# Two modulation loads ahead of the key strips, combined modulations inside the first slot, and the second MLP's rounding and weight split moved

## What is computed

```
x = L0(x, cond): h = LN(x)*(1+scale)+shift; GQA with rope, sparse mask, 16 heads; x + y @ Wo.T
x = L1(x, cond): x + attn(ada_rms(x)) @ Wo.T, 8 query heads, one key head;
                 x + (silu(h @ Wg.T) * (h @ Wu.T)) @ Wd.T,  h = ada_rms(x)
x = L2(x, cond): x + attn(LN(x)*(scale1+1)+shift1) * gamma1, 16 heads, cosine scores;
                 h = gelu((LN(x)*(scale2+1)+shift2) @ Wfc1.T + bfc1)
                 x + (h @ Wfc2.T + bfc2) * gamma2
x = L3(x, cond): x + silu(LN(experts(x))*(1+scale)+shift) @ out_W + out_b
```

## Time and profile before

| | us |
|---|---|
| median of 3 runs | 2375.68 |
| their range | 2372.73 to 2376.46 |
| the profiled execution | 2368.46 |
| its span | 2366.7 |

### The profile page before, as it was taken

One profiled execution on the slowest core, in us unless ns is written; L12 is line 12 of the kernel. 1 busy time (PEld: TensorE's weight loads), 2 busy tenths in 40 slices (PEclk: granted clock), 3 DMA queues, 4 the chain that ended last, 5 costly groups with the idle time before them and its releaser, 6 DMA issues.

```text
span 2366.7 us, 33414 instructions
## 1 busy us (share of the span) xinstructions
PE 2231.2 (94%) x13442; PEld 1492.4 (63%) x13442; DVE 1169.9 (49%) x2498; ACT 1039.6 (44%) x2433; POOL 286.2 (12%) x239
## 2 busy tenths in 40 slices
PE   7789999999999999999999889999999899999998
PEld 2355556545555688888887656565655578888633
DVE  2355455445456434434333467566577454444322
ACT  3365556444345211111113376666676552222473
POOL 2332122112111100010000000001010110000021
PEclk8799999999999999999999999999999999999999
DMA  7411010000000103120002211111110100100001
GB/s 235 158 41 40 24 54 15 28 23 17 25 32 27 58 1 107 45 67 19 27 6 98 81 54 54 37 55 46 45 37 19 54 5 31 36 1 1 1 19 53
DMA packets 60715, 104.93 MB, mean 44 GB/s; under 512 B 10624, under 2 KB 25488, under 8 KB 60560
## 3 DMA queue, kind: packets, MB, share of 16 engines
q1 hardware_dynamic: 60208, 102.37, 13.0%
q0 software_dynamic: 352, 0.42, 0.1%
HBM read 77.07 MB, written 10.49 MB: 37 GB/s over the span
## 4 chain that ended last, share of the span: by engine, by line
PE 84%; ACT 7%; DVE 6%; SPq 1%; DMA 1%; issue 1%; POOL 1%; DVEq 0%; ACTq 0%; POOLq 0%
PE banks L1300 36%; PE banks L408 22%; PE banks L749 6%; PE banks L741 5%; PE banks L765 4%; ACT sb_Pr L888 2%; PE banks L269 1%; PE banks L976 1%; DVE sb_hN L368 1%; ACT sb_PT L893 1%; PE banks L634 1%; PE banks L642 1%; DVE sb_Pr L836 1%; PE banks L960 1%; PE banks L789 1%
## 5 line engine op out<-in xcount | busy, mean ns | idle before, releaser
L1300 PE MATMUL banks<-sb_HH,sb_Ws 128*128 128x512 f32 x1536 | 489.5, 392 | 7.6 <-DVE sb_HL L1188 7.6
L1300 PEld LDWEIGHTS banks<-sb_HH,sb_Ws 128*128 128x128 f32 x1536 | 289.6, 189 | 71.1 <-issue 8.1
L1300 PE MATMUL banks<-sb_hidH,sb_Ws 128*128 128x512 f32 x1024 | 330.3, 392 | 0.4 <-DVE sb_x L1371 0.4
L888 ACT ACTIVATE sb_Pr<-sb_Pr,sb_nmax 128x512 f32<-128x512 f32 (+4 forms) x512 | 291.6, 576 | 20.9 <-DVE sb_nmax L836 20.8
L1300 PE MATMUL banks<-sb_HL,sb_Ws 128*128 128x512 f32 x768 | 299.8, 390 | 0.0
L893 ACT ACTIVATE sb_PT<-banks 128x512 f32<-128x512 f32 (+2 forms) x320 | 144.1, 497 | 291.5 <-PE banks L749 232.5
L843 DVE COPY sb_PT<-banks 128x512 f32<-128x512 f32 (+2 forms) x320 | 168.0, 564 | 169.5 <-PE banks L749 112.0
L749 PEld LDWEIGHTS banks<-sb_ident,sb_Pr 128*128 128x128 f32 x1536 | 168.4, 142 | 125.9 <-issue 35.8
L749 PE MATMUL banks<-sb_ident,sb_Pr 128*128 128x128 f32 x1536 | 213.5, 281 | 18.4 <-DVE sb_A L876 5.0
L1300 PEld LDWEIGHTS banks<-sb_hidH,sb_Ws 128*128 128x128 f32 x1024 | 192.2, 188 | 43.6 <-issue 2.3
L1300 PE MATMUL banks<-sb_hidL,sb_Ws 128*128 128x512 f32 x512 | 199.3, 389 | 0.0
(11 more groups left out here) (164 smaller groups left out, 3178.3 us busy)
## 6 DMA issues: line engine op xcount, KB each, us to landing
sb_ring<-split_units SPq DMA_DIRECT2D x48, 512.0 KB, 3.2
sb_ropet<-sb_R SPq DMA_DIRECT2D x70, 128.0 KB, 2.1
sb_staged<-in_L_cond_Wfc SPq DMA_DIRECT2D x16, 512.0 KB, 4.4
sb_wada<-in_L_cond_Wada SPq DMA_DIRECT2D x6, 1024.0 KB, 5.4
split_units<-sb_unitpair SPq DMA_DIRECT2D x12, 512.0 KB, 2.9
sb_x<-in_x SPq DMA_DIRECT2D x4, 1024.0 KB, 9.1
sb_staged<-in_L_cond_Wg SPq DMA_DIRECT2D x8, 512.0 KB, 3.6
sb_staged<-in_L_cond_Wu SPq DMA_DIRECT2D x8, 512.0 KB, 4.6
```

What stands on the lines that cost most here:

```text
L888: ins = e.activation(prob, prob if s.biased else k.bank(n % 4)[:, 0:s.width(u)], ACT.Exp, bias=s.stat(k, k.nmax, b, u), scale=-1.0 if s.bi ...
L1300: mm = e.matmul(bank, lhsT, rhs, start=i == 0, stop=i == len(mats) - 1)
```

## The change

1. SP loads blocks 8 and 9 ahead of the key strips.
2. The seven `comb` operations and the rounding of `headsel` leave the end of `lead` and are spread over slot 0 as a fourth stream of side work (`sums`). Slot 0 has eight beats more.
3. Batch 1's rounding for the second MLP (`beats((pair2, 1))`) moves from the MLP's first parts to the `closing` of the last attention slot, two beats at each of two points.
4. The second MLP's weight chunk is split in two pieces of 1024 columns, staged in four buffers that are loaded and freed singly. Chunk 1's two pieces stand in two parts, `(2, 4)`. The last slot has one beat more.

```diff
-                ins = e.tensor_copy(high, s.staged[index % 2][:, 0:w])
+                ins = e.tensor_copy(high, s.staged[index % len(s.staged)][:, 0:w])
...
-        staged2 = [place("staged20", 25600, [P, 2048]), place("staged21", 4096, [P, 2048])]
+        staged2 = [place(f"staged2{i}", o, [P, 1024]) for i, o in enumerate((25600, 26624, 4096, 5120))]
...
-            [(ada, 0, "act", "scales", 0)] + [(ada, 0, "dve", "comb", i) for i in range(len(combs))] +             [(headmatrix, 0, "dve", "round", 0)]
+            [(ada, 0, "act", "scales", 0)]
+        sums = [[(ada, 0, "dve", "comb", i)] for i in range(len(combs))] + [[(headmatrix, 0, "dve", "round", 0)]]
...
-            sides01.append(([] if m else pre(1, 0)) + first + among(late, rest, pre(m + 2, 0)) + [[]])
+            sides01.append(([] if m else pre(1, 0)) + first +
+                           among(late, rest, pre(m + 2, 0), *([] if m else [sums])) + [[]])
...
-        mlp2 = mlp(2, False, split2, staged2, [(0, 2 * C * HC)], norm2b, pair2, [("proj2", B - 1, "mm", 11)],
+        mlp2 = mlp(2, False, split2, staged2, [(0, C * HC), (C * HC, 2 * D)], norm2b, pair2, [("proj2", B - 1, "mm", 11)],
...
+        second = beats((pair2, 1))
...
-                           closing=[[], first[0], [], first[1]])
-        hidden2 = fold(parts, (0, 1, extras(0) + extras(1)), (0, 2, beats((pair2, 1))), (0, 4, beats((post2, 3))),
-                       (2, 3, mlp2.split(1)), (1, start[2] + 1, beats((norm2b, 2))),
+                           closing=[[], first[0] + sum(second[:2], []), sum(second[2:], []), first[1]])
+        hidden2 = fold(parts, (0, 1, extras(0) + extras(1)),  (0, 4, beats((post2, 3))),
+                       (2, 4, mlp2.split(1)), (1, start[2] + 1, beats((norm2b, 2))),
...
-            for n in (6, 7):
+            for n in range(6, 10):
                 load_block(n)
...
-                    for n in range(8, len(blocks)):
+                    for n in range(10, len(blocks)):
                         load_block(n)
...
                 if j >= 2:
-                    done("mlp2", 0, "low", j - 2)
+                    done("mlp2", 0, "low", 2 * j - 4)
...
+                if j >= 2:
+                    done("mlp2", 0, "low", 2 * j - 3)
```

More of the change, by code:

```diff
@@ L1507, in conditioned_stack @@
         l_ring = [sem(f"l_ring{i}") for i in range(4)]
-        l_m = [sem(f"l_m{i}") for i in range(2)]
+        l_m = [sem(f"l_m{i}") for i in range(4)]
         s_zero = sem("s_zero")
@@ L1834, in conditioned_stack @@
                           lambda b: [("out3", b - 3, "mm", C - 1)] if b >= 3 else
-                          mlp_down("mlp2", LAST - 3) + [("mlp2", 0, "low", NCH - 1)])
+                          mlp_down("mlp2", LAST - 3) + [("mlp2", 0, "low", 2 * NCH - 1)])
         norm3 = SideNorm("norm3", y3, y3, combc(3), combc(4), eps5[:, 0:1],
@@ L1852, in among3 @@
             return sum(among(*parts), [])
-        l_m_at, seen = {1: [], 2: []}, [0, 0]
-        for layer, loads in ((1, [2, 1] * NCH), (2, [2] * NCH)):
+        l_m_at, seen = {1: [], 2: []}, [0] * 4
+        for layer, count, loads in ((1, 2, [2, 1] * NCH), (2, 4, [1, 1] * NCH)):
             for n, m in enumerate(loads):
-                seen[n % 2] += 16 * m
-                l_m_at[layer].append(seen[n % 2])
+                seen[n % count] += 16 * m
+                l_m_at[layer].append(seen[n % count])
         def up(W, layer_ups):
@@ L1869, in mlp @@
             heads = f"heads{n}"
-            return Mlp(f"mlp{n}", gated, W, pieces, staged, lambda i: (l_m[i % 2], l_m_at[n][i]),
+            return Mlp(f"mlp{n}", gated, W, pieces, staged, lambda i: (l_m[i % len(staged)], l_m_at[n][i]),
                        up(W, 2 if gated else 1), down(W, (2 if gated else 1) * C * HC), norm, pair,
@@ L2094, in _ @@
                     done(*values_end("heads2", 2)[0])
[L2095 to L2098 removed]
+                e.dma_start(staged2[2 * (j % 2)][:].rearrange("p (c m) -> p c m", c=C),
+                            rows("L2_cond_Wfc1")[:, :, j * HC:(j + 1) * HC]).then_inc(l_m[2 * (j % 2)], 16)
+                if j >= 2:
+                    done("mlp2", 0, "low", 2 * j - 3)
+                e.dma_start(staged2[2 * (j % 2) + 1][:].rearrange("p (t m) -> p t m", t=2),
+                            rows("L2_cond_Wfc2")[:, 2 * j:2 * j + 2, :]).then_inc(l_m[2 * (j % 2) + 1], 16)
                 if j == 3:
```

6 lines of the change are left out of this document (1 added, 5 removed).

## The result

The changed kernel took 2358.58 us (median of 6 runs, 2346.25 to 2362.16) against 2373.69 us of the kernel before on the same chip (6 runs). The ratio is 0.9933, with a 95% interval from 0.9918 to 0.9948: 15.9 us less. A second set of six runs on another chip gave 0.9946 (0.9934 to 0.9958), 12.8 us less. The forecast was 2355.8 us, 19.9 us less, a ratio of 0.9916. Both times lie inside the range of 2348 to 2366, and both gains fall short of the forecast, by 4.0 and 7.1 us; the second, 12.8, lies outside the 15 to 25 that the forecast had for itself, and nearer to the 12 of rival (a). Two executions of the experiments are far off the others, 4410 us for p3_round and 2866 us for p1_e_empty_beats, and are in none of the ratios.

The account below looks back on a forecast made before the run. TensorE, busy 94%, was taken as the bound, so only its waits and low-clock stretches count. Gains 14.0 + 0.25 - 0.5 + 5.1 + 1.0 = 19.9 us, from 2375.68 to 2355.8 us; range 2348 to 2366, the forecast's own 2351 to 2361.

Parts of the forecast that it names:

- rival (a): Start gives back more: slow strips, late block 11, or slot 0 bound by GpSimd and dearer sums; gain about 12, 14%.
- Part 1: At the start, TensorE's 10.79 us wait for block 8 goes, block 10 waits 1.3 us; gain 14.0, bounds 11 to 15.3.
- Part 2: First maximum's 3.35 us wait moves to batch 1's mean, gain 0.25; slot 0 loses 0.5, between gain 2 and loss 3.
- signs of being wrong: Strips issued beyond 66 us, low clock after 90, larger wait ending slot 3, or 100 us gain shrunk at 180.
- Part 3: At the attention's end, HL1 wait and clock give 6.8 us, less 1.7 at batch 2's variance; net 5.1, between 3 and 6.8.
- The later wait: In the second MLP, batch 3's wait hangs on batch 2's chain and moves with it; no size of its own given.
- Part 4: In the attention, smaller split pieces shorten the 2.43 us stall; gain 1.0, between gain 2.4 and loss 1; MLP costs nothing.
- the lower bound: In the attention, batch 0's roundings shifted by one beat can make maxima wait for ScalarE; within the loss of 1 us.
- the price of cutting an operation in two: On VectorE, two split pieces cost 0.6 us more than one whole by the rows, 0.3 by the skill's fixed cost.
- The clock rival (d): TensorE's clock stays at 1.2 GHz through slot 0 because of many short waits; +40 us, time 2396, 4%.

Follow-up runs that it names:

- p3_round: Kernel before with only batch 1's rounding moved to the attention's end, chunk 1 still split as one piece: 0.9969 of before, -7.4 us.
- p1_e_empty_beats: Kernel before with blocks 8 and 9 loaded ahead of the strips and eight empty beats in slot 0, sums left ahead of the first maximum: 0.9965, -8.3 us.
- p12: Kernel before with the early loads of blocks 8 and 9 and the sums spread over slot 0, nothing else: 0.9961 of before, -9.3 us.
- after_again: The whole changed kernel run once more, on another chip beside the kernel before: 0.9946 of before.
- p13: Kernel before with the early loads of blocks 8 and 9 and batch 1's rounding moved, without the spread sums and split pieces: 0.9907, -22.1 us.
- p2_sums: Kernel before with only the seven sums and the rounding spread over slot 0, with its added beats: 1.0032 of before, +7.6 us.
- p1_loads: Kernel before with only the loads of blocks 8 and 9 put ahead of the key strips: 0.9941 of before, -14.0 us.

## Why the prediction was right, and where not

**Part 1, right in each step.** Blocks 8 and 9 were issued from 47.47 us on by a queue with nothing else to do, the strips started at 52.15, no later than before, and took 10.93 us. Block 10 was issued behind them at 63.13 and ran at 68.63 after a DMA wait of 1.46 us; the forecast was 1.3 us and 70.0, which is the same once the 1.4 us are taken off by which this execution was ahead at 50 us. Block 11 did not wait. Forecast 14.0, measured 13.9 in the ledger; the 14.0 of the medians has 5 us either way and could not tell 14 from 10. What the forecast did not have is the lower clock behind block 10, which takes 1.5 of the 13.9 us in some executions, the changed kernel's profile among them. (The prediction's 64.51 + 5.4 is 69.91, where it has 69.97; nothing hangs on it.)

**Part 2, the step that failed.** The forecast had a gain of 0.25 at the first maximum and a loss of 0.5 in slot 0, "between a gain of 2 and a loss of 3". The first half is shown: the wait went over to the mean, at 85.84 where 86 was written. The second half was mis-sized. Over the 704 matmuls of slot 0 the changed kernel loses 1.6 us against part 1 alone, p12 3.5 and after_again 6.4, and part 2 alone loses 6.9 against the kernel before; in the times part 2 alone costs 7.6 us (5.0 to 10.2). The prediction did name the mechanism, "TensorE reaches the variance before GpSimd has it", and then let "projection work done earlier" pay for it. It doesn't pay. With empty beats TensorE idles 16.44 us in slot 0 against 14.38 with part 1 alone, 2.06 us more, and the new wait at the variance is 2.01 us: in sum, the work that is pulled forward shortens no other wait. And the clock, which costs little where TensorE waits anyway, is paid in full here.

Two of the signs of being wrong that the prediction lists came: the gain had shrunk between 100 and 180 us, and the clock was low after 90 us (0.50 from 90 to 97 us). The second tells nothing, since p13 without part 2 has the same 0.50 there and loses nothing by it. Rival (a), "the start gives back more", had four clauses. The chain of slot 0 bound by GpSimd is the true one. Sums of over 1 us on VectorE came in part, 0.75 to 1.22 us each where 0.37 was taken from a row of six, but TensorE does not wait for them. Strips issued slowly and block 11 late did not come.

**Part 3, right, and somewhat better.** HL1's last low part was done at 1835.64 in the changed kernel, ten microseconds before TensorE came to it, on VectorE:

```profile
1834.36 1.28 DVE L1188 TENSOR_TENSOR sb_HL<-sb_hN,sb_HH 128x512 fp32r<-128x512 f32 x2
```

The forecast was 6.8 us before the variance wait and 5.1 after it. Alone, with the variance wait unchanged, part 3 gave 7.4 (4.3 to 10.4), and the ledger of p3_round steps by 7.1 between 1850 and 1890. The split's piece ahead of the centring, on VectorE in the changed kernel, against the earlier trace rows:

```profile
1859.14 0.69 DVE L1340 CAST sb_Ws<-sb_staged 128x1024 fp32r<-128x1024 f32 x1
1859.86 1.23 DVE L1344 TENSOR_TENSOR sb_Ws<-sb_staged,sb_Ws 128x1024 fp32r<-128x1024 f32 x1
1861.00 2.47 DVE L348 TENSOR_TENSOR sb_hN<-sb_x,banks 128x512 f32<-128x512 f32 x4
```

cost 1.65 us at the variance (2.60 against 0.95) where 1.7 was written. The forecast booked it under part 3; it is part 4's. The later wait, for batch 3's HL3, did move with the chain and kept its size: 2.24 us, 2.23 before.

**Part 4, mis-sized.** Forecast a gain of 1.0; the attention's side of it gave 0.2 us in the ledger, and with the variance wait part 4 is a loss of about 1.4 by the profiles. The times show no difference (0.9991 to 1.0014, from 2 us gained to 3 us lost). The stall of 2.43 us went further than forecast, wholly; what took its place is the case that stood in the lower bound, batch 0's rounding in front of something that TensorE waits for. Its row is the 2.06 us wait above.

On the price of cutting an operation in two the prediction had 0.6 us of VectorE time a chunk from the first MLP's rows. In the second MLP of the changed kernel, groups by shape:

```profile
L1344 DVE TENSOR_TENSOR sb_Ws<-sb_staged,sb_Ws 128x1024 fp32r<-128x1024 f32 x16 | 19.6, 1225 | 0.6
L1340 DVE CAST sb_Ws<-sb_staged 128x1024 fp32r<-128x1024 f32 x16 | 10.9, 680 | 0.0
```

two pieces take 2 x (0.68 + 1.225) = 3.81 us against 3.51 whole: 0.3 us. The row that I had taken, 1362 ns, was a mean of eight of which seven took 1.22 to 1.23 us and one 2.32, in the kernel before:

```profile
727.93 2.32 DVE L1344 TENSOR_TENSOR sb_Ws<-sb_staged,sb_Ws 128x1024 fp32r<-128x1024 f32 x1
```

The Trainium skill (VectorE: DVE Perf Modes, on the TRN2 errata) gives a fixed cost of 151 cycles at 0.96 GHz for a float32 operation on two tensors, an estimate of 0.31 us for two more instructions; the trace agrees, with 2 x 1.225 - 2.293 = 0.16 us for the subtraction cut in two and 2 x 0.680 - 1.218 = 0.14 us for the cast.

**The sum.** 14.0 + 7.4 - 4.7 - 0.7 = 16.0 us from the medians of part 1, part 3, part 2 on top of part 1, and part 4, against 15.9 measured in the first set. That they agree to 0.1 us is luck: each term has 3 to 5 us either way, and the second set gave 12.8. The forecast's 19.9 was too large by 4.5 us for part 2 and by 1.7 for part 4, and too small by 2.3 for part 3, whose single run does not have the longer variance wait that the forecast took off there; that wait is in part 4's figure. So it is in part luck as well that the forecast was only 4 us off: the error of part 3 took back over a third of the two others. The clock rival (d) did not come as written: the mean clock of slot 0 is 0.81 at the lowest, not 0.50. But its mechanism is in part 2's price: in after_again and in p2_sums TensorE's busy time there is 5.2 and 5.1 us above that of p1_loads and of the kernel before, an eighth of the 40 us, and in the changed kernel's first profile it is 0.3.

## What to carry to other kernels

Before moving small operations off a wait, look at which engine is ready next and by how much: here GpSimd's last sum was done at 99.84 and the mean started at 100.09 us, so taking away the wait of 3.35 us ahead of them could give 0.25 us, and the empty places that the move made in the order cost more than the operations (6.2 us between the two kernels that have one without the other). In an order made of beats, an added beat is a change by itself, to be priced at the neighbours that it shifts. A mean over a few short operations hides what one alone costs: 0.37 us in a row, 0.75 to 1.22 alone. And a load that waits on a queue behind copies of another kind can be put ahead of them, or between them, for as long as its buffer is free and the copies' own reader is far away.
